# A decoder layer on one core: the loop written out, and the second attention rebuilt

## The chip, the cores and the metric

The kernel runs on one core of a Trainium2 chip. TensorE (PE, with its weight loads, PEld), VectorE (DVE), ScalarE (ACT), GpSimd (POOL) and the DMA queue of SyncE (SP) each follow an instruction list of their own and wait for one another through semaphores. The metric is the device time of one launch in microseconds (us). Most executions of one kernel agree within 0.3%.

## The reference

There are 16 sequences (batches) of 256 tokens with 128 features, everything in fp32. Each goes through three blocks, each followed by a residual sum and a layer norm:

```python
x = _layernorm(x + attn(x))            # 16 heads of 64, causal, distance bias, 2 null keys
x = _layernorm(x + xattn(x, ctx))      # the "second attention": 16 heads of 8, 64 context rows
x = _layernorm(x + ffn(x))             # two matrices without a nonlinearity, 8 groups
# xattn:
qh = einsum('bshd,hed->bshe', q, wq) + bq;  kh = ... + bk;  vh = ... + bv
attn = softmax(einsum('bshd,bthd->bhst', qh, kh) / sqrt(8))
out = (attn @ vh) @ wo.T + bo
```

## The kernel before, in words

A sequence is two tiles (t = 0, 1) of 128 tokens. All engines run one software pipeline of 16 turns, `iteration(i, w, g)`. A turn does the first attention of batch i, the projections of batch i+1, the second attention of batch i-1 and the feed-forward of batch i-1. The order of the work on each engine is written out by hand in `iteration`, and it is strict: an engine that waits holds all that stands behind it. `schedule` writes turns 0, 1, 14 and 15 out; turns 2 to 13 are six passes of a device loop (`Fori`) of two turns. In that loop a wait's value is worked out in registers.

The order on PE in one turn i:

- scores of the first attention in fp32 (L579; heads lie on 64-row halves of the array), with `project_v(i, 6..7)` and `project_qk(i+1, 0..3)` between. A projection is three fp32r products of 512 columns (L462 to L464).
- the first probabilities turned (L599) and weighed (L613), then `weigh_nulls(i, 0)` (L624).
- **the middle of the turn**: `cross_scores(i-1, 0..3)` between `project_qk(i+1, 4..7)`, `cross_values(i-1, 0..1)`, `turn_probs(i, 4..5)`.
- `weigh_values(i, 4..11)`, each with a `turn_probs` behind it. In odd turns a product of the two feed-forward matrices stands between.
- **the tail**: `turn_cross_probs(i-1, 0..3)` (L688), `weigh_cross_values(i-1, 0..3)` (L698), `project_v(i+1, 0..2)`, `x1_turn(i)` and `cross_q(i)` (L638), then `turn_qk(i+1)` (L561) between the last `project_v`, `x2_turn`, `feed_forward`.

How the second attention was done. The queries of head h are 8 rows of `xq`. `spread_context` on POOL multiplies the context keys by a mask into `kexp`, and the values into `vexp`, each 128x1024, so that one product gives the scores of 8 heads. Queries and keys are doubled over the partitions (`xw` has each half of the features twice), as a high and a low fp32r part: ACT writes `xqT_hi` (L1378), DVE the rest `xqT_lo` (L1080). A call `cross_scores(b, k)` (t = k // 2, heads half = k % 2) is two fp32r products of 512 columns, L650 and L652, into bank `psS0` or `psS1`. DVE's `cross_shift` takes the maximum and subtracts it (L1093, L1095). ACT's `cross_exponentials` (L1383), DVE's `cross_denominators` (L1100) and POOL's `norm_cross` (L1564) follow. `cross_values` multiplies the spread values by the output matrix (8 products per batch, L662), ACT copies them to `xv` (L1387), and `weigh_cross_values` sums 16 products of 128x128 (L698) straight into y2, which DVE adds (L1107). `kexp` and `vexp` have one buffer each.

On ACT the middle of a turn is in this order: `copy_qk` 4, 5, 6, `cross_exponentials(0)`, `copy_qk` 7, `square_qk(0, 0)` (L1325), `copy_pT(4)`, `cross_exponentials(1)`, `copy_pT(5)`, `square_qk(0, 1)`, `copy_xv` 0 and 1, `copy_pT(7)`. In the tail: `copy_xpT` 0, `qk_seed(1)`, `copy_xpT` 1, the seed of ln2, `copy_v` 0, `copy_xpT` 2, `copy_v` 1, `copy_xpT` 3, `copy_x1T`, `copy_xqT`.

## Time and profile before

| | us |
|---|---|
| median of 3 runs | 1043.22 |
| lowest and highest | 1042.83, 1047.91 |
| the profiled execution's own time | 1046.49 |
| its span | 1044.6 |
| share of PE, DVE, ACT, POOL | 89%, 79%, 65%, 44% |
| granted TensorE clock, mean | 0.971 |

The page gives, for each engine, the union of the times in which it had an instruction running. An fp32 matmul shows as two records, an fp32r one as one. Ends of matmuls are modelled, so the distance from one start to the next says more than a duration. "Idle before, releaser" is what ended the time in which an engine did nothing; "issue" is idle time for which the profile shows no releaser.

### The profile page before, as it was taken

The page shows a single profiled execution, that of the slowest core. Times are in us where ns is not written, and L with a number is a line of the kernel's source. Part 1 is how long each engine was busy: PE and PEld are TensorE (multiplying, and loading weights), DVE is VectorE, ACT ScalarE, POOL GpSimd, SP SyncE. Part 2 cuts the span into 40 slices and gives each one's busy share as a digit, 9 for nine tenths or more (in the row PEclk, how much of TensorE's full clock was granted, in tenths as well). Part 3 has the DMA queues.
Part 4 walks back from the last instruction along what each step waited for, and adds up shares of the span by engine and source line. Part 5 has one row for each costly group of instructions (what it writes and reads, how often), then busy time and mean ns, then how long its engine had stood idle before and what let it go on. Part 6 is the DMA issues. An engine that isn't in the chain of part 4 may idle for free.

```text
span 1044.6 us, 21679 instructions
## 1 busy us (share of the span) xinstructions
PE 926.9 (89%) x6349; PEld 749.4 (72%) x6349; DVE 826.2 (79%) x2595; ACT 673.8 (65%) x1970; POOL 457.8 (44%) x356
## 2 busy tenths in 40 slices
PE   6887998989899898998979899798989989999785
PEld 5666686868768686786858778586876868777574
DVE  7757788887779877898878888689777987878655
ACT  4764767676575765757667575667747676775642
POOL 0253361826327172552816346172642727264341
PEclk9999999999989998999999999899999999999896
DMA  6000000001000010000100001000010000000000
GB/s 190 6 1 11 1 26 12 6 7 27 14 6 7 11 27 9 7 6 12 26 9 6 12 6 27 14 5 8 8 32 7 7 11 22 6 6 6 6 1 11
DMA packets 26289, 16.24 MB, mean 16 GB/s; under 512 B 3872, under 2 KB 25376, under 8 KB 26144
## 3 DMA queue, kind: packets, MB, share of 16 engines
q1 hardware_dynamic: 26144, 14.52, 4.8%
q8 instruction: 65, 1.06, 0.4%
q14 instruction: 80, 0.66, 0.2%
HBM read 12.41 MB, written 2.10 MB: 14 GB/s over the span
## 4 chain that ended last, share of the span: by engine, by line
PE 51%; DVE 22%; issue 11%; ACT 10%; POOL 3%; DMA 2%; DVEq 0%; ACTq 0%; SPq 0%; POOLq 0%
PE psY L613 11%; PE psS L579 7%; PE psT L599 5%; ACT pr L1353 5%; PE psJ L462 4%; PE psJ L464 3%; PE psJ L463 3%; POOL pr L1557 3%; PE psS L561 3%; PE psS L652 2%; PE psS L698 2%; DVE pr L1029 2%; DVE ssq L982 2%; ACT sq L1325 2%; PE psJ L662 2%
## 5 line engine op out<-in xcount | busy, mean ns | idle before, releaser
L1557 POOL TENSOR_TENSOR pr<-pr,rden 128x512 f32<-128x512 f32 x192 | 193.3, 1040 | 394.1 <-DVE rden L1044 343.9
L1353 ACT ACTIVATE pr<-pr,nmin 128x256 f32<-128x256 f32 (+1 forms) x512 | 225.5, 444 | 12.4 <-DVE nmin L1029 11.7
L1029 DVE CUSTOM_DVE_ANT_0 pr<-psS,alibi,nullmin 128x256 f32<-128x256 f32 (+1 forms) x512 | 183.7, 414 | 46.0 <-PE psS L579 43.2
L613 PE MATMUL psY<-val,pT 128*128 128x128 f32 x1536 | 205.8, 280 | 13.0 <-DVE pT L1053 8.6
L613 PEld LDWEIGHTS psY<-val,pT 128*128 128x128 f32 x1536 | 187.0, 193 | 19.4 <-DVE pT L1053 10.6
L1548 POOL TENSOR_TENSOR qk<-qk,rn 128x1024 f32<-128x1024 f32 x64 | 121.2, 1915 | 85.0 <-DVE x L895 49.6
L579 PE MATMUL psS<-kT,qT 64*128 64x256 f32 (+1 forms) x1024 | 117.9, 363 | 31.6 <-issue 17.4
L599 PE MATMUL psT<-ident,pr 128*128 128x128 f32 x768 | 119.5, 279 | 21.2 <-POOL pr L1557 21.2
L579 PEld LDWEIGHTS psS<-kT,qT 64*128 64x128 f32 x1024 | 82.6, 203 | 62.8 <-DVE nmin L1029 30.8
L599 PEld LDWEIGHTS psT<-ident,pr 128*128 128x128 f32 x768 | 87.9, 142 | 41.4 <-POOL pr L1557 35.6
L1353 ACT ACTIVATION_READ_ACCUMULATOR pr<-pr,nmin 128x1 f32 x512 | 97.1, 190 | 0.0
L1338 ACT ACTIVATE val<-psJ 128x512 f32<-128x512 f32 x112 | 66.3, 594 | 44.7 <-PE psJ L464 42.4
L1368 ACT ACTIVATE pT<-psT 128x512 f32<-128x512 f32 x112 | 66.0, 590 | 23.9 <-PE psT L599 23.1
L462 PE MATMUL psJ<-wqk_hi,xnT_hi 128*128 128x512 f32 x128 | 61.0, 476 | 20.5 <-DVE xnT_lo L976 19.1
L982 DVE TENSOR_REDUCE ssq<-sq 128x16 f32<-128x1024 f32 x64 | 76.3, 1212 | 2.2 <-ACT sq L1325 1.7
L1093 DVE TENSOR_REDUCE xmax<-psS 128x8 f32<-128x512 f32 x64 | 44.0, 688 | 42.7 <-PE psS L652 42.7
L1403 ACT ACTIVATE xpT<-psT 128x512 f32<-128x512 f32 x64 | 37.8, 594 | 61.9 <-PE psT L688 60.6
L1317 ACT ACTIVATE qk<-psJ 128x512 f32<-128x512 f32 x80 | 47.6, 594 | 39.4 <-PE psJ L464 37.6
L1053 DVE COPY pT<-psT 128x512 f32<-128x512 f32 x80 | 54.5, 682 | 19.9 <-PE psT L599 18.8
L698 PEld LDWEIGHTS psS<-xv,xpT 128*128 128x128 f32 x512 | 64.5, 194 | 5.6 <-issue 1.3
L561 PE MATMUL psS<-ident,qk 128*128 128x128 f32 x512 | 67.7, 275 | 0.0
L698 PE MATMUL psS<-xv,xpT 128*128 128x128 f32 x512 | 66.0, 277 | 1.2 <-issue 1.0
(138 smaller groups left out, 1876.2 us busy)
## 6 DMA issues: line engine op xcount, KB each, us to landing
w1s<-w1b SPq DMA_DIRECT2D x8, 258.0 KB, 2.9
xin<-x SPq DMA_DIRECT2D x16, 128.0 KB, 2.2
xres<-x SPq DMA_DIRECT2D x16, 128.0 KB, 2.1
w2s<-w2T SPq DMA_DIRECT2D x8, 256.0 KB, 3.1
out<-x SPq DMA_DIRECT2D x16, 128.0 KB, 1.9
pr<-w_q SPq DMA_DIRECT2D x1, 512.0 KB, 4.3
pr<-w_kv SPq DMA_DIRECT2D x1, 512.0 KB, 4.7
pr<-wvT SPq DMA_DIRECT2D x1, 512.0 KB, 4.1
```

Of the source, the lines that this page charges most:

```text
L462: pe.matmul(dst, hi, whi, start=True, stop=False)
L561: mm = pe.transpose(psS[isk][:, P * j:P * (j + 1)], qk[t][:, col:col + P], ident[:])
L579: mm = pe.matmul(psS[score_bank(t, c)][:, keys * j:keys * (j + 1)], qT[r, h // 2, P * t:P * (t + 1)], kT[r, h // 2, 0:keys], start=True, s ...
L599: mm = pe.transpose(psT[c % 2][:, P * j:P * (j + 1)], pr[t][:, h, P * kt:P * (kt + 1)], ident[:])
L613: mm = pe.matmul(psY[t], pT[c % 4][:, P * j:P * (j + 1)], val[:, kt, P * h:P * (h + 1)], start=(blk == 0), stop=False)
L698: mm = pe.matmul(psS[2][:, P * t:P * (t + 1)], xpT[half][:, P * j:P * (j + 1)], xv[:, 4 * half + j, :], start=(half == 0 and j == 0), stop ...
L982: steps.mark(dve.tensor_reduce(ssq[:, t, H * half:H * (half + 1)], sq[:, HD * half:HD * (half + 1)].rearrange("p (h d) -> p h d", d=DH), A ...
L1029: dve.tensor_tensor_reduce(pr[t][:, h, :], psS[score_bank(t, c)][:, keys * j:keys * (j + 1)], alibi[:, h, SEQ - keys:SEQ], 1.0, nullmin[:, ...
L1338: act.activation(val[:, c // 4, 512 * (c % 4):512 * (c % 4) + 512], psJ[c % 2][:], ACT.Copy).then_inc(v_copied_act, 1)
L1353: act.activation(pr[t][:, h, :], pr[t][:, h, :], ACT.Exp, bias=nmin[:, t, h:h + 1], scale=-1.0, accum_out=dparts[:, t, h, 0:1]).then_inc(e ...
L1548: pool.tensor_tensor(v, v, rn[:, t, H * k:H * (k + 1)].unsqueeze(2).broadcast_to([P, H, DH]), ALU.mult).then_inc(qk_normed, 1)
L1557: pool.tensor_tensor(pr[t][:, hs, :], pr[t][:, hs, :], rden[:, t, hs].unsqueeze(2).broadcast_to([P, heads, P * (t + 1)]), ALU.mult).then_i ...
```

## The change

Two things are changed together. First, `schedule` writes all 16 turns out; no engine has a loop, and all waits are on constants. Second, the second attention is rebuilt:

- Queries and keys stay once over the partitions (8 heads in rows 0 to 63, 8 in rows 64 to 127). `cross_q` is one product, `copy_xqT` one copy, `split_xqT` on DVE is gone. `kexp` is 128x512.
- `cross_scores(b, t)` is two fp32 products on the two row halves, into `psS0` and `psS1`. It needs both banks free.
- `cross_values` and `copy_xv` are gone. `vexp` is 128x256 in two buffers: for each pair of heads a block of 32 columns. `weigh_cross_values(b, t)` is 8 products with 32 weight columns and 128 moving columns, each writing 32 partitions of the bank `psS2`. It waits for both `copy_xpT` of its tile.
- `copy_xoT` on ACT (128x256, after `copy_x1T`) and `merge_cross_heads` on PE (two 128x128 products with the output matrix, after `cross_q`) come ahead of `add_y2`.
- `context_kv` in turn 0 makes the keys with 2 products and the values with 32 small ones, without DVE's `split_context_k`. `shape_of_pairs` writes a mask with five memsets on DVE before turn 0. Three more small DMAs stand in the start.

```diff
-            for i in range(FIRST):
-                iteration(i, i % 2 == 1, (i - 1) // 2)
-            with eng.Fori(0, TURNS) as turn:
-                if steps:
-                    steps.enter_loop(turn, per_turn)
-                for half in range(2):
-                    iteration(2 * turn + (FIRST + half), half == 1, turn + half)
+            for i in range(NB):
+                iteration(i, i % 2 == 1, (i - 1) // 2)
...
             def context_kv():
+                for k in range(2):
+                    take(f'J{k}', kvx_copied, k + 1)
+                    pe.matmul(psJ[k][:], xw[:, 1, :], ctxT_s[:, 512 * k:512 * (k + 1)],
                               start=True, stop=True).then_inc(kvx_ready, 1)
+                for k in range(4):
+                    take(f'J{k % 2}', kvx_copied, k + 3)
+                    for j in range(4):
+                        col = slice(CTX * (4 * k + j), CTX * (4 * k + j + 1))
+                        for half in range(2):
+                            mm = pe.matmul(psJ[k % 2][CTX * half:CTX * (half + 1), P * j:P * (j + 1)],
+                                           ctxT_s[:, col], xw[:, 2, :], start=True, stop=True)
+                    mm.then_inc(kvx_ready, 1)
...
+                pe.matmul(psJ[1][:, 0:SEQ], xw[:, 0, :], x1T[:], start=True, stop=True).then_inc(xqT_ready, 1)
+            def cross_scores(b, t):
+                if t == 0:
+                    pe.wait_ge(xqT_copied, b + 1)
+                    pe.wait_ge(kexp_ready, b + 1)
                 for half in range(2):
+                    take(f'S{half}', xs_sub, XC * b + 2 * t + half + 1)
                 tok = slice(P * t, P * (t + 1))
-                pe.matmul(psS[half][:], xqT_hi[:, half, tok],
-                          kexp[:, half, :, :].rearrange("p h k -> p (h k)"), start=True, stop=False)
-                pe.matmul(psS[half][:], xqT_lo[:, half, tok],
-                          kexp[0:DH, half, :, :].rearrange("p h k -> p (h k)"),
-                          start=False, stop=True).then_inc(xscores_ready, 1)
-            def cross_values(b, c):
-                for j in range(4):
-                    p = 4 * c + j
-                    mm = pe.matmul(psJ[c][:, P * j:P * (j + 1)],
-                                   vexp[:, 2 * p:2 * p + 2, :].rearrange("p h k -> p (h k)"), xwo[:],
-                                   start=True, stop=True)
+                for half in range(2):
+                    r = slice(DH * half, DH * (half + 1))
+                    pe.matmul(psS[half][:], xqT[r, tok], kexp[r, :, :].rearrange("p h k -> p (h k)"),
+                              start=True, stop=True).then_inc(xscores_ready, 1)
...
+            def weigh_cross_values(b, t):
+                if t == 0:
+                    pe.wait_ge(vexp_ready, b + 1)
                     take('S2', h2_added, b + 1)
+                pe.wait_ge(xpT_copied, XC * b + 2 * t + 2)
+                for r in range(2):
+                    for j in range(XH // 4):
+                        mm = pe.matmul(psS[2][32 * j:32 * (j + 1), SEQ + P * t:SEQ + P * (t + 1)], vexp[b % 2][:, j, r, :],
+                                       xpT[j // 2][:, P * (2 * (j % 2) + r):P * (2 * (j % 2) + r + 1)],
+                                       start=(r == 0), stop=(r == 1))
                 mm.then_inc(xpv_done, 1)
+            def merge_cross_heads(b):
+                pe.wait_ge(xoT_copied, b + 1)
+                for t in range(NT):
+                    mm = pe.matmul(psS[2][:, P * t:P * (t + 1)], xoT[:, P * t:P * (t + 1)], xwo[:],
+                                   start=True, stop=True)
+                mm.then_inc(y2_ready, 1)
...
                 if c:
                     cross_scores(i - 1, 0)
                 if a:
                     project_qk(i + 1, 4)
                     project_qk(i + 1, 5)
                     project_qk(i + 1, 6)
                 if c:
+                    cross_scores(i - 1, 1)
                 if a:
                     project_qk(i + 1, 7)
...
                         project_v(i + 1, k)
                     if k == 2:
                         cross_q(i)
+                    if c and k == 0:
+                        weigh_cross_values(i - 1, 0)
+                        turn_cross_probs(i - 1, 2)
+                        turn_cross_probs(i - 1, 3)
+                    if c and k == 1:
+                        weigh_cross_values(i - 1, 1)
                     if k == 1:
                         x1_turn(i)
+                    if c and k == 3:
+                        merge_cross_heads(i - 1)
...
-                split_xqT(i)
...
+            def copy_xoT(b):
+                act.wait_ge(xpv_done, NT * (b + 1))
+                act.activation(xoT[:], psS[2][:, SEQ:2 * SEQ], ACT.Identity, bias=xb[:, 2:3]).then_inc(xoT_copied, 1)
...
                 need(pool, xscores_ready, XC * b)
+                pool.tensor_tensor(kexp[:], hmask2[:].unsqueeze(2).broadcast_to([P, XHALF, CTX]),
+                                   kTx[:, col].unsqueeze(1).broadcast_to([P, XHALF, CTX]),
                                    ALU.mult).then_inc(kexp_ready, 1)
+                need(pool, xpv_done, NT * (b - 1))
+                pool.tensor_tensor(vexp[b % 2][:], xwide[:],
+                                   vx[:, row, :].rearrange("p o (j f) -> p (o j) f", f=32).unsqueeze(2)
+                                   .broadcast_to([P, XH // 4, 2, 32]), ALU.mult).then_inc(vexp_ready, 1)
```

## Rows read from the trace of the kernel before

**Rows 1.** The page: busy time, share of the span and instructions of each engine.
```profile
PE 926.9 (89%) x6349; PEld 749.4 (72%) x6349; DVE 826.2 (79%) x2595; ACT 673.8 (65%) x1970; POOL 457.8 (44%) x356
```
**Rows 2.** Windows from score start to score start: length, busy per engine, granted clock.
```profile
159.78:219.24 59.46, 54.76 (x387) 44.38 (x387) 51.30 (x161) 41.07 (x120) 28.61 (x22) 1.00 0.03 8
219.24:841.94 622.70, 565.73 (x3910) 458.59 (x3911) 510.48 (x1601) 413.83 (x1215) 286.11 (x220) 0.98 0.05 13
841.94:902.17 60.23, 56.01 (x396) 45.60 (x397) 50.74 (x161) 41.65 (x123) 28.63 (x22) 1.00 0.06 17
902.17:961.41 59.24, 54.36 (x386) 44.67 (x387) 48.67 (x151) 40.85 (x118) 28.53 (x22) 1.00 0.02 6
1004.60:1044.60 40.00, 24.96 (x138) 20.65 (x137) 21.96 (x69) 11.45 (x27) 5.99 (x5) 0.80 0.02 7
```
**Rows 3.** Timeline of PE, first loop end: start, length, instruction, idle before.
```profile
282.55 1.16 PE L579 MATMUL psS<-kT,qT 64*128 64x128 f32 x16 [3.36 <-issue]
```
**Rows 4.** Timeline of PE, middle of turn 14.
```profile
920.03 1.13 PE L579 MATMUL psS<-kT,qT 64*128 64x256 f32 x8
921.10 0.66 PE L599 MATMUL psT<-ident,pr 128*128 128x128 f32 x4
...
923.94 0.50 PE L650 MATMUL psS<-kexp,xqT_hi 128*128 128x512 f32 x1
...
924.79 0.50 PE L462 MATMUL psJ<-wqk_hi,xnT_hi 128*128 128x512 f32 x1
...
932.87 1.06 PE L613 MATMUL psY<-val,pT 128*128 128x128 f32 x8
...
943.27 2.05 PE L613 MATMUL psY<-val,pT 128*128 128x128 f32 x16 [1.27 <-DVE pT L1053]
```
**Rows 5.** Timeline of PE, tail of turn 13.
```profile
887.77 1.05 PE L698 MATMUL psS<-xv,xpT 128*128 128x128 f32 x8
888.66 0.60 PE L688 MATMUL psT<-ident,xp 128*128 128x128 f32 x4
...
892.34 1.10 PE L638 MATMUL psJ<-x1T,xw 128*128 128x256 f32 x4
893.28 1.95 PE L698 MATMUL psS<-xv,xpT 128*128 128x128 f32 x16
895.06 1.04 PE L561 MATMUL psS<-ident,qk 128*128 128x128 f32 x8
```
**Rows 6.** Timeline of DVE, middle of turn 14.
```profile
924.90 0.69 DVE L1093 TENSOR_REDUCE xmax<-psS 128x8 f32<-128x512 f32 x1 [1.66 <-PE psS L652]
...
927.58 0.69 DVE L1095 TENSOR_TENSOR xp<-psS,xmax 128x512 f32<-128x512 f32 x1
...
931.88 0.69 DVE L1095 TENSOR_TENSOR xp<-psS,xmax 128x512 f32<-128x512 f32 x1
...
940.56 1.83 DVE L884 SCALAR_TENSOR_TENSOR newt<-newt,ssq 128x32 f32<-128x32 f32 x1
```
**Rows 7.** Timeline of ACT, middle of turn 14.
```profile
930.10 1.05 ACT L1325 ACTIVATE sq<-qk 128x1024 f32<-128x1024 f32 x1
...
933.57 0.58 ACT L1368 ACTIVATE pT<-psT 128x512 f32<-128x512 f32 x1
```
**Rows 8.** Timeline of POOL, middle of turn 14.
```profile
938.57 3.77 POOL L1564 TENSOR_TENSOR xp<-xp,xrden 128x1024 f32<-128x1024 f32 x2
```
**Rows 9.** Groups by line and shape: count, busy us, mean ns, idle before.
```profile
L1557 POOL TENSOR_TENSOR pr<-pr,rden 128x512 f32<-128x512 f32 x192 | 193.3, 1040 | 394.1 <-DVE rden L1044 343.9 <-ACT pr L1353 50.2
L1578 POOL TENSOR_TENSOR kexp<-hmask,kTx 128x1024 fp32r<-128x1024 f32 x16 | 30.4, 1903 | 2.7 <-ACT vTx L1310 2.7
```
**Rows 10.** Timeline of ACT, tail of turn 13.
```profile
887.80 0.58 ACT L1403 ACTIVATE xpT<-psT 128x512 f32<-128x512 f32 x1
```
**Rows 11.** Timeline of DVE, tail of turn 13.
```profile
894.96 0.86 DVE L1080 SCALAR_TENSOR_TENSOR xqT_lo<-psJ,xb,xqT_hi 64x256 fp32r<-64x256 f32 x2
...
896.08 0.67 DVE L1019 COPY qT<-psS 128x512 f32<-128x512 f32 x1
```

More of the change, by code:

```diff
@@ L84, in value @@
     def value(self):
-        return self.n + self.offset
+        return self.n
     def wait(self, eng):
         eng.wait_ge(self.sem, self.value())
-    def enter_loop(self, i, per_turn):
-        self.offset, self.before, self.per_turn = i * per_turn, self.n, per_turn
-    def leave_loop(self, turns):
-        assert self.n - self.before == self.per_turn, ("steps of a turn", self.n - self.before)
-        self.n, self.offset = self.before + turns * self.per_turn, 0
 def chunks_to(chunks, n, c):
@@ L201, in program @@
         x1T = sb("x1T", [P, SEQ])
-        xqT_hi = sb("xqT_hi", [P, 2, SEQ], F32R)
-        xqT_lo = sb("xqT_lo", [DH, 2, SEQ], F32R)
-        kexp = sb("kexp", [P, 2, XHALF, CTX], F32R)
-        vexp = sb("vexp", [P, XH, CTX])
-        xv = sb("xv", [P, XH // 2, P])
+        xqT = sb("xqT", [P, SEQ])
+        kexp = sb("kexp", [P, XHALF, CTX])
+        vexp = [sb(f"vexp{k}", [P, XH // 4, 2, 32]) for k in range(2)]
+        xoT = sb("xoT", [P, SEQ])
         xmax = sb("xmax", [P, NT, XH])
@@ L690, in turn_cross_probs @@
                 mm.then_inc(xprobsT_ready, 1)
-            def weigh_cross_values(b, k):
-                t, half = k // 2, k % 2
-                pe.wait_ge(xpT_copied, XC * b + k + 1)
-                if k == 0:
+            def weigh_cross_values(b, t):
+                if t == 0:
+                    pe.wait_ge(vexp_ready, b + 1)
                     take('S2', h2_added, b + 1)
-                for j in range(4):
-                    mm = pe.matmul(psS[2][:, P * t:P * (t + 1)], xpT[half][:, P * j:P * (j + 1)],
-                                   xv[:, 4 * half + j, :], start=(half == 0 and j == 0),
-                                   stop=(half == 1 and j == 3))
-                mm.then_inc(xpv_done, 1)
+                pe.wait_ge(xpT_copied, XC * b + 2 * t + 2)
[4 more added lines that the diff above has]
+                                       start=(r == 0), stop=(r == 1))
+                mm.then_inc(xpv_done, 1)
+            def merge_cross_heads(b):
[4 more added lines that the diff above has]
+                mm.then_inc(y2_ready, 1)
             def x2_turn(b):
@@ L779, in iteration @@
                     project_qk(i + 1, 4)
+                    project_qk(i + 1, 5)
+                    project_qk(i + 1, 6)
                 if c:
@@ L782, in iteration @@
                 if a:
-                    project_qk(i + 1, 5)
-                    project_qk(i + 1, 6)
-                if c:
-                    cross_scores(i - 1, 2)
-                if a:
                     project_qk(i + 1, 7)
-                if c:
-                    cross_values(i - 1, 0)
-                    cross_scores(i - 1, 3)
-                else:
+                if not c:
                     context_kv()
                 turn_probs(i, 4)
-                if c:
-                    cross_values(i - 1, 1)
                 turn_probs(i, 5)
@@ L835, in iteration @@
                         feed_forward(i - 1, g)
-            schedule(pe, iteration)
+            schedule(iteration)
             b = NB - 1
-            for k in range(XC):
-                cross_scores(b, k)
-            cross_values(b, 0)
+            for t in range(NT):
+                cross_scores(b, t)
             x2_turn(b - 1)
-            cross_values(b, 1)
             feed_forward(b - 1, GROUPS - 1)
@@ L847, in _ @@
             turn_cross_probs(b, 1)
-            pe.wait_ge(h2_added, b)
-            for k in range(4):
-                weigh_cross_values(b, k)
-                if k < 2:
-                    turn_cross_probs(b, k + 2)
+            weigh_cross_values(b, 0)
+            turn_cross_probs(b, 2)
+            turn_cross_probs(b, 3)
+            weigh_cross_values(b, 1)
+            merge_cross_heads(b)
             x2_turn(b)
@@ L1376, in copy_xqT @@
                 act.wait_ge(xqT_ready, b + 1)
-                for half in range(2):
-                    act.activation(xqT_hi[:, half, :], psJ[1][:, SEQ * half:SEQ * (half + 1)], ACT.Identity,
-                                   bias=xb[:, half:half + 1]).then_inc(xqT_copied, 1)
+                act.activation(xqT[:], psJ[1][:, 0:SEQ], ACT.Identity, bias=xb[:, 0:1]).then_inc(xqT_copied, 1)
             def cross_exponentials(b, t):
@@ L1506, in iteration @@
                 copy_x1T(i)
+                if c:
+                    copy_xoT(i - 1)
                 copy_xqT(i)
@@ L1536, in _ @@
                 copy_xpT(b, k)
+            copy_xoT(b)
             ln_seed("ln3", (0, 1), NB)
```

138 lines of the change are left out of this document (45 added, 93 removed).

## The prediction

> **What bounds the kernel now.** I read the page's busy times first [rows 1]: PE is busy 89% of the span, DVE 79%. So the change, which takes work mostly off PE, looks like a large gain. Then I cut the span into turns, from the first score product of one to that of the next [rows 2]. Turn 2, an even turn in the loop that no loop end touches, takes 59.46 us; turn 13, odd, in the loop and also with no loop end behind it, takes 60.23. Turn 14 is written out and takes 59.24. The reader is to see that PE is busy only 54.4 to 56.0 of these, at full clock: some 4 us per turn are PE waits, mostly for DVE, and DVE's own 50 us are in one chain with them. The third view is the time line of each engine in the middle and in the tail of a turn [rows 4 to 8, 10, 11]. There I follow which wait would end last when PE's part gets shorter.
>
> **Part 1, the loop.** The ten turns 3 to 12 take 622.70 us together [rows 2]. Five odd and five even ones without a loop end would take 5 x (60.23 + 59.46) = 598.45. The difference, 24.25 us, is the price of five loop ends, 4.9 each. PE stands 3.36 us at the first of them with no releaser ("issue") [rows 3], and the rest comes behind it: the mean granted clock of the stretch is 0.98 where the turns beside it have 1.00 [rows 2]. Written out, this goes. Bounds: at least 5 x 3.36 = 17, if the lost clock came back for other reasons; at most 25 plus the register work. Of that I find next to nothing: turn 14 (written out, without the load for i+2) is 0.22 shorter than turn 2. I take 0.07 for 12 turns, so 1. The price of the longer code is bounded by the same rows: turn 14 is straight-line code and shows no stall. I take -25.
>
> **Part 2, PE's work in the second attention.** Per turn, from start to start. A `cross_scores` call was 0.85 (923.94 to 924.79) [rows 4], four of them 3.4. The new one has two fp32 products of 512 columns on two row halves. The nearest row is a pair of score chunks: four products of 256 columns on the same halves in 1.07 (920.03 to 921.10) [rows 4], the same columns. Without overlap a record of 256 columns costs 0.235 (four in 0.94, `cross_q`, 892.34 to 893.28) [rows 5], so 8 x 0.235 = 1.9. I take 1.07, since it is the same form, so 2.1 for two. `cross_q` falls from 0.94 to 0.47. `weigh_cross_values` was four times 0.89 (887.77 to 888.66) [rows 5], 3.6, and `cross_values`, eight products of that size, adds 1.8. The new weighing has 8 products of 128 columns per tile: 8 x 0.22 = 1.78 if the four column groups take turns, a quarter of it, 0.45, plus some 0.2 for entering and leaving, if they run side by side. No row shows 32-column weights side by side. I take 0.65, by analogy with the row halves, and keep 1.78 as the other end. `merge_cross_heads` costs two products, 0.45. Sum: 3.4 + 0.94 + 3.6 + 1.8 = 9.7 before, 2.1 + 0.47 + 1.3 + 0.45 = 4.3 after. PE loses 5.4 us of work per turn, 80 us in 15 turns. I expect most of it to turn into waits.
>
> At this place the Trainium skill speaks for and against. "TensorE: Matmul & The Clock Gate" (Part 3, packing small matmuls) states 2.38 times for three column tiles of 32, but also that weight loads overlap running matmuls only when the row group differs, and here all column groups share all rows. By the first, a tile would cost 1.78 / 2.38 = 0.75, an estimate; by the second, 1.78. No run here shows either yet.
>
> **The middle of the turn** (turn 14's times). `cross_scores(0)` starts at 923.94 as before and ends both halves at 925.0, so DVE's first shift starts at 925.1 instead of 924.90 [rows 6]. First shift, denominators and second shift take until 928.4 as DVE's own work (the second ended at 928.27, 927.58 + 0.69 [rows 6]). PE has done `project_qk` 4 to 6 by 927.2 and waits, since `cross_scores(1)` needs both banks: 1.2 us idle. It runs 928.5 to 929.6. Shift 3 then ends about 932.5 (before: 931.88 + 0.69 = 932.57 [rows 6]). `project_qk(7)` ends 930.4. Behind it ACT has, in order, `copy_qk` 7, the squares (1.05 [rows 7]) and `copy_pT(4)`: it ends 932.6, and `weigh_values(4)`, which was at 932.87 [rows 4], starts at 932.65. `cross_exponentials(1)` waits for shift 3, so `copy_pT(5)`, at 933.57 before [rows 7], starts at 933.55. So the 3 us that PE saves here come out as 0.05: two PE waits, 1.2 and 1.4 us. Bounds: +0.9 if the two row halves don't overlap, -2.5 if ACT and DVE had the slack that I don't find.
>
> Then PE is paced by its own weighing until it waits 1.27 for the copy of pT(10) [rows 4]. DVE is late there because its Newton step L884 takes 1.83 (940.56 to 942.39), ending with POOL's two-instruction normalization (938.57 + 3.77 = 942.34) [rows 6, 8]. It is that POOL work which holds it. POOL's `kexp` falls from 1.90 to about 1.04, the price of 128x512 [rows 9], and `vexp` by more. But `norm_cross` waits for DVE's reciprocals, which come some 0.35 earlier (`copy_pT(6)` earlier, since PE's second `cross_values` no longer stands ahead of its transposes). I take -0.35 for this stage, bounds -1.3 (the whole wait goes) and +0.6.
>
> **The tail** (turn 13's times). `weigh_cross_values(0)` now waits for both copies of its tile. The second ends at 887.80 + 0.58 = 888.38 [rows 10], so PE starts at 888.4 instead of 887.77 [rows 5]; 0.65 of work, then both transposes 0.9, 890.0; `project_v(1)` to 890.7. Behind it, on ACT: `copy_v` 1 to 891.3, `copy_xpT` 3 to 891.8. `weigh_cross_values(1)` runs 891.85 to 892.5, then `x1_turn`, `project_v(2)`, `cross_q` (893.9) and the merge (894.3; ACT's two copies ahead of it are done by 893.6). `turn_qk` starts at 894.3 instead of 895.06 [rows 5]. DVE had `split_xqT` for 0.86 [rows 11] ahead of `add_y2` and the first qT copy: without it the copy can start at 895.3, not 896.08 [rows 11]. Both engines agree on -0.75. With column groups one after the other the two weighings cost 2.3 more, of which nothing is hidden: 896.6, so +1.6 instead.
>
> **The sum.** Turns 1 to 14: 14 x (-0.05 - 0.35 - 0.7) = -15. The last 40 us, the chain of the last batch [rows 2]: `split_xqT`, the output product with both `copy_xv`, and part of the weighing at half clock leave it; the merge and `copy_xoT` come in: -3, bounds 0 and -6. Start and turn 0: DVE's splits of the keys and of xqT go, five memsets and 32 small value products (32 x 0.22 = 7 us if none overlap) come in: -1, bounds -4 and +3. Together -25 - 15 - 3 - 1 = -44, against the profiled execution's 1046.5: 1002.5. That execution lay 3.3 above the median. Should the loop ends have cost more in it than in the others, the new kernel has none; otherwise the median is to be scaled. I take 1001.
>
> **The rivals.**
> - Column groups take turns, as the second rule says. For it: no row shows otherwise. Against: the row halves do overlap. The tail is 2.3 worse per turn, 14 x 2.3 = 33: about 1035, from 1028 to 1045.
> - In between: weight loads set the pace, 1.0 per tile, between the two ends. The tail loses 0.7 of its 0.75, 10 us, and start and end 4 more: 1016.
> - PE's saving is realized. For it: PE is the busiest engine [rows 1]. Against: the chains above. If 2.2 more of the 5.4 us came through per turn, 1001 - 31 = 970.
> - Slower: the clock. PE now waits in four more places of each turn, 4 to 5 us in all. In the last 40 us, where PE is busy 62%, the granted clock is 0.80 [rows 2]; in full turns, with 93%, it is 1.00. If each turn gets a stretch at 1.2 GHz behind the waits of the middle and one in the tail, as each loop end has (4.9 less the 3.36 of standing still is 1.5, where only the scores stage is hit), and these reach the dense weighing of 10 us, which at half speed takes 10 more, the turn loses up to 10. It decides from 3 us per turn on, 14 x 3 = 42: then nothing is gained. At 4 us: 1057. Against it: no new wait is longer than 1.5 us, and in the steady turns waits of 1.3 us leave the clock at 1.00.
>
> **Chances.** Forecast 55% (own range 990 to 1012), the in-between 15%, taking turns 14%, PE's saving 10%, clock 6%. The range reaches from the case of 970 to the middle of the taking-turns case: 972 to 1037. A measurement tells 0.5%, 5 us, from no change. Faster than that: all of the forecast, the in-between and PE's saving, and 9 of the 14 for taking turns, 0.89. Same 0.05, slower 0.06.
>
> **What would show it.** No 3 us "issue" gap on PE. Turns of about 58.2. PE busy near 50 us per turn with more idle time, ended by DVE's xp (L1095) ahead of the second cross scores, by ACT's pT ahead of weigh 4, by ACT's xpT ahead of both cross weighings. Weighing starts eight products within 0.5 to 0.7 us if the column groups overlap, within 1.8 if not. The forecast is wrong if `weigh_values(4)` comes over 1 us earlier after `weigh_nulls(0)` than the 8.9 of before, or if the granted clock of full turns is below 1.00.

## The result and the profile after

The changed kernel takes 1009.24 us (median of 5 runs, 1008.33 to 1014.34) against 1045.45 (median of 5) for the kernel before: a ratio of 0.967, 95% interval 0.965 to 0.970. The forecast was 1001, faster. The profiled execution of the changed kernel is the longest of its five, 1014.34 us with a span of 1012.2; the one of before had 1044.6. All times inside the programs below are from such profiled executions, which scatter by some 5 us, most of it before turn 1 (below).

The page first: engines with busy us, share and instructions [rows 1 has before].

```profile
PE 849.9 (84%) x6181; PEld 663.4 (66%) x6181; DVE 802.7 (79%) x2564; ACT 660.7 (65%) x1938; POOL 425.7 (42%) x356
```

PE has lost 77 us of work, twice what the kernel has gained. Windows from score start to score start: turn 2, turns 3 to 12, turn 13, turn 14, turn 15, and what lies behind it (columns as in [rows 2]).

```profile
164.49:222.90 58.41, 49.99 (x373) 39.09 (x373) 50.11 (x159) 40.27 (x118) 26.60 (x22) 1.00 0.03 8
222.90:810.74 587.84, 506.41 (x3771) 396.87 (x3771) 495.70 (x1581) 405.46 (x1195) 266.09 (x220) 1.00 0.05 12
810.74:869.89 59.15, 51.29 (x382) 40.31 (x383) 49.02 (x159) 40.80 (x121) 26.61 (x22) 1.00 0.06 17
869.89:928.31 58.42, 49.95 (x372) 39.09 (x373) 47.43 (x149) 39.96 (x116) 26.56 (x22) 1.00 0.02 6
928.31:980.12 51.81, 39.37 (x294) 30.86 (x294) 28.97 (x113) 27.02 (x93) 17.50 (x16) 0.90 0.01 4
980.12:1012.20 32.08, 14.28 (x72) 8.59 (x72) 18.78 (x56) 7.38 (x17) 5.97 (x5) 0.55 0.03 8
```

Against [rows 2]: turns 3 to 12 fell from 622.70 to 587.84, which is ten plain turns (5 x (58.41 + 59.15) = 587.8); nothing of a loop end is left. A plain even turn fell by 1.05, an odd one by 1.08, though PE works 4.7 us less in each; its idle time rose from 4.7 to 8.4 us. Added up over the span: turns 1 to 14 gave 38.4 us (24.3 for the loop ends, 14.1 for the rest of the turns, of which the first experiment gives some 4 to the loop). All before turn 1 took 5.3 more (105.4 against 100.1), turn 15 and what follows 0.7 more (83.9 against 83.2).

The middle of turn 14 on PE, as in [rows 4], 32.4 us earlier on the clock of the profile:

```profile
891.55 1.13 PE L636 MATMUL psS<-kexp,xqT 64*128 64x512 f32 x4
...
896.22 1.13 PE L636 MATMUL psS<-kexp,xqT 64*128 64x512 f32 x4 [1.00 <-DVE xp L1061]
...
900.45 1.13 PE L600 MATMUL psY<-val,pT 128*128 128x128 f32 x8 [1.33 <-ACT pT L1334]
...
910.70 2.05 PE L600 MATMUL psY<-val,pT 128*128 128x128 f32 x16 [1.09 <-DVE pT L1028]
```

The saved work has become the two waits that were forecast, 1.00 and 1.33 us, and the third wait is still there. The tail of the same turn:

```profile
915.39 0.65 PE L672 MATMUL psS<-xpT,vexp 128*32 128x128 f32 x16 [0.51 <-ACT xpT L1367]
915.97 1.09 PE L660 MATMUL psT<-ident,xp 128*128 128x128 f32 x8
...
918.93 0.64 PE L672 MATMUL psS<-xpT,vexp 128*32 128x128 f32 x16 [1.18 <-ACT xpT L1367]
...
921.47 1.04 PE L548 MATMUL psS<-ident,qk 128*128 128x128 f32 x8
```

Sixteen records, the eight products of a cross weighing, take 0.58 us from start to start (915.39 to 915.97). Both waits for xpT are there. DVE in the middle and the tail of turn 14, beside [rows 6 and 11]:

```profile
907.90 1.92 DVE L859 SCALAR_TENSOR_TENSOR newt<-newt,ssq 128x32 f32<-128x32 f32 x1
...
917.06 1.90 DVE L976 TENSOR_TENSOR nullneg<-nullmul,nullbias 128x64 f32<-128x64 f32 x1
...
920.76 0.69 DVE L989 COPY val<-psJ 128x512 f32<-128x512 f32 x1 [1.56 <-PE psJ L443]
...
927.05 0.69 DVE L994 COPY qT<-psS 128x512 f32<-128x512 f32 x1 [0.98 <-PE psS L548]
```

The Newton step (L859, L884 of before) is as long as it was. In the tail it is now DVE that waits for PE (1.56 and 0.98 us).

### The profile page after: what moved, and what is told of

It reads as the page before. It is cut to its first block, busy times and chain, and to the rows that moved or that the text cites. A ratio compares the mean times of both kernels' runs of the same rounds, so it can differ in the third digit from the quotient of the medians.

```text
span 1012.2 us, 18717 instructions
## 1 busy us (share of the span) xinstructions
PE 849.9 (84%) x6181; PEld 663.4 (66%) x6181; DVE 802.7 (79%) x2564; ACT 660.7 (65%) x1938; POOL 425.7 (42%) x356
## 4 chain that ended last, share of the span: by engine, by line
PE 45%; DVE 25%; ACT 18%; issue 6%; POOL 4%; DMA 2%; DVEq 0%; ACTq 0%; POOLq 0%
PE psY L600 12%; ACT pr L1319 9%; PE psS L566 6%; PE psT L586 5%; PE psS L636 4%; ACT sq L1291 3%; POOL pr L1519 3%; PE psJ L441 3%; PE psS L548 3%; PE psJ L443 2%; PE psJ L442 2%; DVE xp L1061 2%; DVE xmax L1059 2%; DVE ssq L957 2%; ACT xpT L1367 2%
## 5 line engine op out<-in xcount | busy, mean ns | idle before, releaser
L1319 ACT ACTIVATE pr<-pr,nmin 128x256 f32<-128x256 f32 (+1 forms) x512 | 225.3, 443 | 10.8 <-DVE nmin L1004 10.2
L600 PEld LDWEIGHTS psY<-val,pT 128*128 128x128 f32 x1536 | 186.6, 193 | 41.8 <-issue 22.2
L586 PE MATMUL psT<-ident,pr 128*128 128x128 f32 x768 | 116.9, 279 | 20.2 <-POOL pr L1519 20.2
L566 PE MATMUL psS<-kT,qT 64*128 64x256 f32 (+1 forms) x1024 | 111.7, 346 | 19.3 <-DVE nmin L1004 12.9
L566 PEld LDWEIGHTS psS<-kT,qT 64*128 64x128 f32 x1024 | 78.2, 189 | 48.5 <-DVE nmin L1004 19.4
L1304 ACT ACTIVATE val<-psJ 128x512 f32<-128x512 f32 x112 | 66.5, 594 | 25.6 <-PE psJ L443 25.1
L1526 POOL TENSOR_TENSOR xp<-xp,xrden 128x1024 f32<-128x1024 f32 x32 | 60.9, 1902 | 29.2 <-DVE xrden L1068 28.5
L441 PEld LDWEIGHTS psJ<-wqk_hi,xnT_hi 128*128 128x128 f32 x128 | 24.9, 195 | 65.1 <-issue 31.5
```

Source lines behind the costliest of these rows:

```text
L441: pe.matmul(dst, hi, whi, start=True, stop=False)
L566: mm = pe.matmul(psS[score_bank(t, c)][:, keys * j:keys * (j + 1)], qT[r, h // 2, P * t:P * (t + 1)], kT[r, h // 2, 0:keys], start=True, s ...
L586: mm = pe.transpose(psT[c % 2][:, P * j:P * (j + 1)], pr[t][:, h, P * kt:P * (kt + 1)], ident[:])
L600: mm = pe.matmul(psY[t], pT[c % 4][:, P * j:P * (j + 1)], val[:, kt, P * h:P * (h + 1)], start=(blk == 0), stop=False)
L1304: act.activation(val[:, c // 4, 512 * (c % 4):512 * (c % 4) + 512], psJ[c % 2][:], ACT.Copy).then_inc(v_copied_act, 1)
L1319: act.activation(pr[t][:, h, :], pr[t][:, h, :], ACT.Exp, bias=nmin[:, t, h:h + 1], scale=-1.0, accum_out=dparts[:, t, h, 0:1]).then_inc(e ...
```

## The experiments

Each was timed beside the kernel before on one chip; the ratio is to that. Where turns are given, they are read as windows from score start to score start in the run's own profile; from turn 2 to turn 13 they repeat within 0.05 us, even with even and odd with odd, but for a single odd one in some of the kernels. Two of the kernels, one column group and the quarter of the normalization, leave out part of the result; they serve for their times alone.

**The loop alone.** The kernel before with its loop written out.

```
-            with eng.Fori(0, TURNS) as turn:
-                for half in range(2):
-                    iteration(2 * turn + (FIRST + half), half == 1, turn + half)
+            for i in range(NB):
+                iteration(i, i % 2 == 1, (i - 1) // 2)
```

> The kernel before with only its loop over the batches written out; the second attention as it was. My sum has the five loop ends at 24.3 us: their stall of 3.4 us and a stretch at the lower clock behind each, and next to nothing for registers. That gives 24 to 26 us below the kernel before, about 1020, with turns 3 to 12 as long as the others (60.2 odd, 59.5 even), no 3 us gap of PE without a releaser, and the start of turn 1 where it was (100.1 us). Rival A: the longer code costs instruction fetches; then the gain is under 20 us and gaps without a releaser are spread over the turns. Rival B: the start of the changed kernel (5.3 us later at turn 1) is due to the written-out program and not to the second attention: then turn 1 begins 3 to 5 us later here too.

1019.48 us, ratio 0.974 (0.970 to 0.978). Turn 2, turns 3 to 12, turn 13, and turn 15 with all behind it:

```profile
163.20:222.48 59.28, 54.53 (x387) 44.52 (x387) 51.23 (x161) 41.10 (x120) 28.59 (x22) 1.00 0.03 8
222.48:817.62 595.14, 551.33 (x3911) 451.25 (x3911) 506.19 (x1601) 413.77 (x1215) 285.88 (x220) 1.00 0.04 12
817.62:877.36 59.74, 55.73 (x396) 45.73 (x397) 49.98 (x161) 41.62 (x123) 28.58 (x22) 1.00 0.06 17
936.50:1018.10 81.60, 60.26 (x392) 48.58 (x392) 48.53 (x170) 35.79 (x113) 25.50 (x21) 0.85 0.02 6
```

By the medians the loop is 26 of the 36 us. The loop ends are the 24.3 of the forecast, and the plain turns are shorter too, 0.18 even and 0.49 odd against [rows 2], some 4 us where I had 1. I put that down to the register work, the only difference in those turns that I can name; no run separates it. The second attention's edits are then worth 10 us: a pair of turns goes from 119.02 to 117.56, 1.46 less. It lies in the tail (last null weighing to next score start, 16.30 and 16.22 to 15.63); the middle (first to last null weighing) fell by 0.19 in even turns and by nothing in odd ones. Turn 1 begins at 103.6, as in rival B. But seven of the nine profiles listed under the start below, all of written-out kernels, have it between 99.6 and 102.3, so the written-out program alone does not make it 3 to 5 us late.

**One column group.** All products of a cross weighing in the first 32 columns; three quarters of the attended values are left uncomputed.

```
-                for r in range(2):
-                    for j in range(XH // 4):
-                        mm = pe.matmul(psS[2][32 * j:32 * (j + 1), SEQ + ...
+                for j in range(XH // 4):
+                    for r in range(2):
+                        mm = pe.matmul(psS[2][0:32, SEQ + ...
```

> The changed kernel, but the eight products of a cross weighing all go to the first 32 columns of the array, so that none can run beside another (the three other quarters of the attended values are left uncomputed). If the column groups are what makes the weighing 0.58 us from start to start, it becomes 1.7 to 1.8 us per tile, two tiles per turn, and since the tail of a turn is now bound by PE all of it shows, less what covers a wait of 0.5 or 1.2 us: the second wait (1.18) comes from ACT, which also moves later, so +2.0 to +2.4 us per turn, 28 to 34 us in all, about 1040, the same as the kernel before. Rival: the weight loads and not the products set the pace, then a tile takes 0.9 to 1.1 and the kernel 1018 to 1024. Rival 2: such small products cost little in either arrangement, then 1009.

1048.52 us, ratio 1.003 (1.000 to 1.005): slower than the kernel before by a hair. First the two groups of the weighing by line (count, busy us, mean ns, idle before), this kernel's and then the changed kernel's; then this kernel's turn 14.

```profile
L672 PE MATMUL psS<-xpT,vexp 128*32 128x128 f32 x512 | 63.1, 278 | 26.5 <-ACT xpT L1367 26.5
```

```profile
L672 PE MATMUL psS<-xpT,vexp 128*32 128x128 f32 x512 | 21.5, 287 | 26.5 <-ACT xpT L1367 26.5
```

```profile
898.89:959.88 60.99, 52.53 (x372) 41.61 (x373) 47.43 (x149) 40.00 (x116) 26.57 (x22) 1.00 0.02 5
```

A record takes the same 280 ns in both; only their overlap differs. The two weighings of a turn take 1.84 and 1.87 us from start to start instead of 0.58 each, 2.55 more together; the turn is 2.57 longer, all of it in the tail (15.63 to 18.20). So nothing hides the weighing, and the column groups are what makes the rebuilt attention pay: without them it gives back all that the loop had won. "TensorE: Matmul & The Clock Gate" of the Trainium skill (Part 3, "Measured speedup vs the span model") gives 2.38 times for three column tiles; four gave 1.87 / 0.58 = 3.2 here, and the weight loads did not force them one after the other, although all groups share their rows.

**ACT's copy of pT(4) first.**

```
                     copy_qk(i + 1, 7)
-                    square_qk(i + 1, 0, 0)
...
                 copy_pT(i, 4)
+                if a:
+                    square_qk(i + 1, 0, 0)
```

> The changed kernel with ACT's copy of pT(4) ahead of the first squares (1.05 us) instead of behind them. PE's weighing of chunk 4 waits 1.33 us for that copy in every turn. Theory: the middle of a turn is held at its end by DVE and POOL (Newton step blocked until POOL's normalization ends, then the copy of pT(10)), so the 1.0 us won at chunk 4 is given back as a longer wait at chunk 10 (1.09 us becomes about 1.9), and the squares come later for DVE: 0 to -3 us in all, 1006 to 1009. Rival: ACT's order is what ate PE's saving in the middle; then -0.7 to -1.0 us per turn, 10 to 14 us, 996 to 999. Rival 2: the first squares, 0.6 us later, make DVE's sums and the norms late: 0 to +8.

1009.20 us, ratio 0.964 (0.961 to 0.967); turns 58.42 and 59.17, unchanged. PE in turn 14:

```profile
895.59 1.13 PE L600 MATMUL psY<-val,pT 128*128 128x128 f32 x8 [0.39 <-ACT pT L1334]
...
897.99 1.16 PE L600 MATMUL psY<-val,pT 128*128 128x128 f32 x8 [0.84 <-ACT pT L1334]
...
906.77 2.05 PE L600 MATMUL psY<-val,pT 128*128 128x128 f32 x16 [1.08 <-DVE pT L1028]
```

PE's wait of 1.33 us fell to 0.39, and already the next weighing took it back, with a new wait of 0.84 for ACT's copy of pT(5). The wait for pT(10) stayed (1.08 for 1.09), so the theory had the wrong place for it. The copy of pT(5) stands behind the same work of ACT in both orders, the squares and the second exponentials. The place of this one copy is worth nothing; whether ACT's order as a whole ate the middle's saving was not tried.

**A quarter of the normalization.** POOL normalizes the weights of a quarter of the heads; the others stay as they are.

```
-                    pool.tensor_tensor(xp[t][:], xp[t][:], xrden[:, t, :]...
+                    h = XH // 4
+                    pool.tensor_tensor(xp[t][:, 0:h], xp[t][:, 0:h], xrden[:, t, 0:h]...
```

> The changed kernel with POOL's normalization of the second attention's weights cut to a quarter of the heads (the other three quarters stay unnormalized), so that POOL's two instructions take about 1.2 us instead of 3.85. Theory: it is these that hold DVE's Newton step (1.92 us instead of about 0.2) and so the copy of pT(10); PE's wait of 1.09 us there goes, the turn ends 1.0 us earlier: -14 us, about 995. Rival: the wait passes to the next one in line, PE's own weighing or ACT's copy of pT(11): then -0.3 per turn or less, 1005 to 1009.

999.79 us, ratio 0.957 (0.952 to 0.962): -9.4. DVE in turn 14:

```profile
895.35 0.19 DVE L859 SCALAR_TENSOR_TENSOR newt<-newt,ssq 128x32 f32<-128x32 f32 x1
895.58 0.49 DVE L861 SCALAR_TENSOR_TENSOR rn<-newt,seedq 128x32 f32<-128x32 f32 x1
```

and in turn 13:

```profile
837.62 0.19 DVE L857 TENSOR_TENSOR newt<-seedq 128x32 f32<-128x32 f32 x1 [1.50 <-ACT seedq L1247]
```

Even turns fall to 57.27 (-1.14), odd ones stay at 59.17. So POOL's normalization does hold the middle, but of even turns only. In odd ones DVE waits 1.50 for ACT's seed, which stands behind the copies of the merged feed-forward weights. I had read the middle in turn 14 alone and multiplied by 14.

**The normalization in halves**, four instructions of 512 elements.

```
-                    pool.tensor_tensor(xp[t][:], ...)
+                    for hs in (slice(0, XHALF), slice(XHALF, XH)):
+                        last = pool.tensor_tensor(xp[t][:, hs], ...)
```

> The changed kernel with POOL's normalization of the cross weights in four instructions of 512 elements instead of two of 1024: the same work, about 1.04 us each, 4.1 instead of 3.85 in all. The kernel with a short normalization ran its even turns in 57.27 us instead of 58.41 and its odd ones as before, where DVE waits for ACT's seed instead. Theory: a small DVE operation can begin at an instruction's end of POOL, so DVE's Newton step, which took 1.92 us and ended with POOL's second instruction, takes 1.0 or less, and the even turns become 57.3 to 57.9: -4 to -8 us in all, 1001 to 1005. Rival: POOL keeps DVE out across its back-to-back instructions until it goes idle, then the step is as long as before or longer by 0.2: 1009 to 1011.

1009.45 us, ratio 0.965 (0.963 to 0.968).

```profile
907.91 0.97 DVE L859 SCALAR_TENSOR_TENSOR newt<-newt,ssq 128x32 f32<-128x32 f32 x1
908.91 0.97 DVE L861 SCALAR_TENSOR_TENSOR rn<-newt,seedq 128x32 f32<-128x32 f32 x1
```

The first sentence of the theory holds: the step ends with one instruction of POOL, after 0.97. But each of the two DVE operations behind one another waits for one, so both together are as long as before and the turn gains 0.03.

**ACT's copy of xpT(3) ahead of the value copy.**

```
+                if c:
+                    copy_xpT(i - 1, 3)
                 if a:
                     copy_v(i + 1, 1)
-                if c:
-                    copy_xpT(i - 1, 3)
```

> The changed kernel with ACT's copy of the fourth block of turned cross weights (xpT 3) ahead of its copy of the value chunk (copy_v 1). The second cross weighing waits 1.18 us for that copy in every turn, and the tail of a turn is now bound by PE and this copy, no longer by DVE (DVE's qT copy waits for PE). Theory: the weighing comes about 0.6 us (one ACT copy) earlier and what follows it on PE too, since nothing else waits for copy_v 1 but x1_turn, which stands behind the weighing: -0.4 to -0.6 per turn, -6 to -9 us, 1000 to 1003. Rival: DVE holds the end of the turn (its two copies of qT, the third norm's sums between them), then the saving becomes a longer wait in front of the last transposes: 1007 to 1009.

1005.81 us, ratio 0.963 (0.959 to 0.967). Even turns -0.10, odd ones -0.19, but turn 14 -1.00. That is 2.9 in turns 1 to 14; the medians alone, with intervals that overlap, would not tell it. PE in the tail of turn 12:

```profile
794.40 0.64 PE L672 MATMUL psS<-xpT,vexp 128*32 128x128 f32 x16
...
797.07 1.04 PE L548 MATMUL psS<-ident,qk 128*128 128x128 f32 x8
...
799.43 1.09 PE L548 MATMUL psS<-ident,qk 128*128 128x128 f32 x8 [0.62 <-DVE qT L994]
```

The wait for xpT(3) is gone and PE wins 1.0 us up to the transposes, then waits 0.62 for DVE's first qT copy and is slowed behind it. Theory and rival both hold in part: by what came through, PE and DVE end the tail within 0.2 us of each other. In turn 14, which has no batch i+2 to normalize, DVE has the slack and the whole 1.0 comes through.

**PE's value projection into the wait.**

```
-                    if a and k < 3:
+                    if a and k < 2:
                         project_v(i + 1, k)
+                    if a and k == 1:
+                        project_v(i + 1, 2)
```

> The changed kernel with PE's third value projection (0.7 us of work) in front of the second cross weighing instead of behind it, so that PE has work in the 1.18 us in which it waits for ACT. Theory: the tail is bound by PE's own work plus this wait; -0.5 to -0.7 per turn up to cross_q, less what cross_q then waits for ACT's copy of x1 (0.3 to 0.4): -0.3 per turn, -4 us, about 1005; with no cover by ACT the full -0.7, 999. Rival: DVE or ACT hold the end of the turn, then 1009.

1009.18 us, ratio 0.965 (0.963 to 0.968), turns 58.42 and 59.16: nothing. The work filled the wait (1.18 to 0.48), but the weighing's place is set by ACT's copy, and behind x1_turn a new wait of 0.56 for x1T stands where the projection was.

**One buffer for the spread values.**

```
+            def spread_values(b):
+                need(pool, xpv_done, NT * b)
...
+                spread_values(i)
                 x1_plus_bias(i)
```

> The changed kernel with one buffer of spread values instead of two; POOL fills it late in the turn (0.73 us), in front of its addition of the bias to x1, where it has been free since the weighing of the batch before. Theory: the second buffer is there so that the filling may stand ahead of the normalization on POOL (with one buffer in that place POOL would wait for a weighing that waits for POOL itself); POOL has 1.5 us of idle time in front of both the normalization (it waits for DVE's reciprocals) and the place where it goes, so both cost nothing: 1007 to 1011, even and odd turns 58.4 and 59.2. Rival: the filling in front of the normalization makes it late; then one buffer, filled late, is faster by up to 0.7 us in the even turns, 1004 to 1006.

1010.0 us, ratio 0.967 (0.964 to 0.970), no different from the changed kernel; even turns 58.29, 0.12 shorter, odd 59.15. The second buffer is worth nothing where POOL can fill late; it bought only the place.

**The end with idle products.**

```
+            def keep_busy(n):
+                for _ in range(n):
+                    pe.matmul(psY_bank[:, 2 * P:4 * P], ident[:], alibi[:, 0, :], start=True, stop=True)
```

> The changed kernel with idle products (fp32, 256 columns, 0.47 us each at full clock, into an unused part of a bank) in front of PE's long waits in turn 15 and behind it: 6 and 6 in the turn, 6, 1, 5, 1, 1, 1, 6, 1 behind it. In the profile the last 29 us ran wholly at 1.2 GHz and two stretches in turn 15 too, right behind waits of 3.1 and 3.5 us. Theory (this is why the end gave +0.7 instead of my -3): work in place of the waits keeps the granted clock at 2.4 GHz, the transposes, weighings and merges behind turn 15 (9.5 us of PE time on the path at half clock) take half and some 3 to 5 us in the turn come back: -5 to -8 us, 1001 to 1004. Rival: the end is set by DVE, ACT and POOL, the clock of PE is worth 1 us or nothing there, and the filling that overlaps real work costs: 1008 to 1012.

1003.26 us, ratio 0.961 (0.958 to 0.965): -6. Turn 15 and all behind it, in two windows:

```profile
922.48:971.27 48.79, 40.86 (x319) 32.53 (x319) 28.97 (x113) 27.04 (x93) 17.52 (x16) 1.00 0.01 4
971.27:999.90 28.63, 18.54 (x116) 12.53 (x116) 18.77 (x56) 7.05 (x17) 5.99 (x5) 0.96 0.03 10
```

In the changed kernel these were 51.81 at 0.90 and 32.08 at 0.55. Eight transposes of the last batch took there

```profile
991.27 1.97 PE L660 MATMUL psT<-ident,xp 128*128 128x128 f32 x8 [2.55 <-POOL xp L1526]
```

and here

```profile
981.47 1.09 PE L660 MATMUL psT<-ident,xp 128*128 128x128 f32 x8 [1.15 <-POOL xp L1542]
```

So 5.5 to 6.7 us of the end (77.4 against 82.9 to 84.0 in the profiles of the changed kernel and of the variants that leave the end as it is) are the clock: work that does nothing, put into waits, pays there.

In time the rebuilt attention won nothing there: 82.9 to 84.0 us, against 83.2 in the kernel before and 81.6 in the loop-only kernel, where I had 3 less. The granted clock fits. Over turn 15 and all behind it the mean was 0.86 in the kernel before and 0.85 in the loop-only one, which is 23 and 24 us at 1.2 GHz; in the changed kernel it was 0.77, 39 us. PE is busy for 16.2, 14.2 and 22.2 us of these slow stretches. The products take about half as long at the full clock (the transposes above, 1.97 and 1.09), so the clock costs the changed kernel 3 to 4 us more than the two others, an estimate from these figures and about what is missing. The old attention with a filled end was not run.

**The start.** The fills of the pattern first on DVE, and five idle products ahead of the first transposes.

```
+            shape_of_pairs()
             ln1_begin(0)
...
+            for _ in range(5):
+                pe.matmul(psY_bank[:, 2 * P:4 * P], xoT[:, 0:P], xoT[:], start=True, stop=True)
             pe.wait_ge(c_loaded, 16 * 2)
```

> The changed kernel with two edits at its start: the five fills of the block pattern run on DVE in its first 2.8 us, where it waits for the input, not behind the first qT copies; and PE runs five idle fp32 products of 256 columns on a zeroed tile before the first transposes, where it waits for the input until 5.7 us. In the profile of the changed kernel the first projections have 0.43 us from start to start until 17.3 us and 0.24 behind it, and DVE's first mask is 2.1 us late for PE in turn 0. Turn 1 started at 105.4 there but between 99.7 and 101.4 in five other profiles with the same start, so most of my miss at the start is that one execution. Theory: the early products bring the faster clock to the first projections, and turn 1 starts at 96 to 99; the earlier fills give 0.5 to 1.0 us; 1003 to 1006. Rival A: the start is bound by the loads of the weights and DVE's splits: 1007 to 1009. Rival B: products ahead of the real ones push them back at the lower clock: 1010 to 1012.

1007.13 us (1007.07 to 1007.99), ratio 0.964 (0.962 to 0.966): -2.1, less than expected, and the interval overlaps that of the changed kernel. What speaks for a gain is one profile: turn 1 starts at 98.97. With the unedited start it started at 105.4, 101.4, 101.0, 99.7, 101.1, 101.7, 105.5, 99.6 and 102.3 in the profiles of the changed kernel and its variants (the one with a late fill of the values among them). So my miss of 5.3 us is mostly the one execution; their median is 101.4, 1.2 above the only profile of before. (The expectation named five of them and left out 105.5.) What differs between them is the granted clock: the two at 105.4 and 105.5 have 23.9 us at 1.2 GHz before turn 1, the two at 101.7 and 102.3 have 17.1 and 13.7, the other five 10.2; the kernel before had 6.8 and the loop-only kernel 13.7. Turn 0 is 59.73 instead of 60.56 to 62.8; which of the two edits gave it was not separated.

**Three orders.** The copy of xpT(3) as above; DVE's copy of pT(10) ahead of its Newton steps; POOL's second normalization of q and k behind DVE's null scores.

```
+                copy_pT(i, 10)
                 if a:
                     norms(i + 1, 0)
-                copy_pT(i, 10)
...
-                    pool.wait_ge(x1_ready, i + 1)
+                    pool.wait_ge(dve_step, nulls_at[i + 1])
                     norm_qk(i + 1, 1)
```

> The changed kernel with three changes of order and no change of work: ACT's copy of xpT 3 ahead of its copy of the value chunk 1 (as before, alone -3 us), DVE's copy of pT(10) ahead of the Newton steps of the first norms, and POOL's second normalization of q and k waits until DVE has its null scores instead of starting with x1. Alone the first won PE 1.0 us and gave 0.6 to 0.8 of it back as a wait for DVE's first qT copy, since DVE stands 1.0 and 1.6 us in two small operations that end with POOL's. Theory: DVE comes 2.6 us earlier to the value copy, so the tail keeps its 1.0 us, and in even turns the copy of pT(10) no longer stands behind the blocked Newton step, another 1.0: even turns 56.3 to 57.0, odd ones 58.0 to 58.4, -14 to -21 us, 988 to 995. Rival: POOL is now later at its end and the transposes of the second tile of q and k (turn_qk 4) wait for it: even 57.5, odd 58.4, 999 to 1003.

991.73 us, ratio 0.950 (0.948 to 0.952): 17.5 less than the changed kernel, with no work removed; 13.3 of them lie in turns 1 to 14. The three orders were not timed one by one, but for the first. DVE's null scores in turn 13:

```profile
840.78 0.17 DVE L854 TENSOR_SCALAR ln_ve<-ln_mv 128x2 f32<-128x2 f32 x1
...
841.12 0.23 DVE L977 TENSOR_TENSOR nullneg<-nullmul,nullbias 128x64 f32<-128x64 f32 x1
```

and those of the changed kernel's turn 13:

```profile
859.17 1.23 DVE L853 TENSOR_SCALAR ln_ve<-ln_mv 128x2 f32<-128x2 f32 x1
...
860.56 1.81 DVE L976 TENSOR_TENSOR nullneg<-nullmul,nullbias 128x64 f32<-128x64 f32 x1
```

Even turns take 57.33, odd ones 58.3. In odd turns the tail falls to 14.76, in even ones the middle to 20.40, and there the tail stays at 15.67 against the expectation. The row that says why, PE in turn 12, with DVE's late operation ahead of ACT's seed:

```profile
780.45 0.64 PE L673 MATMUL psS<-xpT,vexp 128*32 128x128 f32 x16 [1.57 <-ACT xpT L1369]
```

```profile
777.71 1.59 DVE L964 TENSOR_SCALAR ssq<-ssq 128x32 f32<-128x32 f32 x1
```

POOL's normalization of q and k now runs beside that DVE operation; ACT computes a seed from it and has the copy of xpT(1) queued behind the seed. To put that copy first is the next edit; it was not tried.

**All together.**

> The three changes of order, the filled end (alone -6 us) and the two edits at the start in one kernel. Theory: places apart from each other add up: the orders' gain, -6, and what the start gives, -3 to -5; 978 to 988. Rival: they share waits, above all in turn 15 and turn 0, and the sum is short by 3 us or more: 990 or over.

986.43 us (985.82 to 987.03), ratio 0.944 (0.942 to 0.945), 22.8 below the changed kernel. The parts are 17.5, 6.0 and 2.1, together 25.6; 2.8 are shared. The three orders alone had already brought turn 1 to 98.4 and turn 15 with all behind it to 81.6; here they are 97.9 and 77.4. It is the fastest kernel of the study.

## Why the prediction was right, and where it was off

- **Loop ends, -24.3**: as forecast, from the windows of [rows 2] alone. What the loop costs beside its ends was mis-sized: 1 us forecast, about 4 measured. I read it from one even turn beside turn 14; odd turns lose more (0.49 against 0.18).
- **Column groups, 0.65 per tile**: 0.58. The rival in which they take turns is refuted for this kernel and confirmed as a price: its tail was forecast 1.6 longer than before, and the kernel that forces it is 1.7 longer (18.19 against 16.46). Its time was forecast at about 1035 (1028 to 1045) and came to 1048.5: my sum lacks 8 us anyway, one group costs 2.57 a turn where I had 2.3, and turn 15 with all behind it takes 88.0 us against 83.9.
- **The middle**: both waits came with their forecast places and sizes (1.0 and 1.33 for 1.2 and 1.4). The -0.35 at pT(10) was too much: -0.19 in even turns, 0 in odd ones, where ACT's seed ends the wait and not POOL. Here is the largest part of the miss in the turns.
- **The tail, -0.7**: -0.6. That it ends on both engines at once was right: with PE's wait alone removed a turn wins 0.1 to 0.2, with ACT's, DVE's and POOL's orders changed together the odd turns' tail wins 0.9.
- **Start and end, -4 together**: failed. The end gave nothing. The filled end shows that the clock costs the changed kernel 5.5 to 6.7 us there, with PE's last 32 us at 0.55; that its growth took the whole 3 is argued from the slow stretches above, not shown. I had counted the work removed at half clock, not that the clock can be lower for longer without it. The start, forecast 1 shorter, is 1.2 longer in the median of profiles; the single execution that I compare with has 5.3.
- **The clock rival (turns at 1.2 GHz behind new waits)**: refuted in turns 2 to 14, granted clock 1.00 with waits up to 1.34 us. It was right in kind for turn 15 and the end.
- **PE's saving realized (970)**: of the 4.5 to 4.7 us that PE works less per turn, some 0.7 came through; the rest of the 1.05 is the loop's.

The sum, with these: 1046.5 - 24.3 - 14.1 + 1.2 + 0 = 1009.3 against 1009.24 measured. That it meets to 0.1 is chance, since start and end scatter by 1 us and more between profiles and 1046.5 is one execution. The forecast of 1001 lacked 8: the end 3, the start 2, the turns 2, and the 1.5 that I took off for the median. The 2 for the turns is luck in part: the loop gave 28.3 where I had 25, the rebuilt attention 10 where I had 15, and the two errors nearly cancel.

## What to carry to other kernels

Take turns with different contents apart before multiplying: an even and an odd turn here wait for different engines at the same place, and one of them gave nothing. When an engine's work is removed, list the waits that remain and whose they are; here the orders on ACT, DVE and POOL were worth 17.5 us, more than the whole rebuilt attention. At a kernel's end, where the busiest engine often waits, read its granted clock: less work on it brought nothing here, and idle products in its waits brought 6 us.

## What the runs showed of the hardware

- Eight fp32 products on four column groups that share all 128 rows take 0.58 us, against 1.84 to 1.87 in one group.
- A small DVE operation that meets a running POOL instruction ends with that instruction (1.92 for 0.19 us, 0.97 when the instruction is half as long), and the next one behind it meets the next instruction. Not all are held: the statistics (two in 0.48), the copies out of PSUM (0.69) and the sums over 1024 elements (1.21) run beside POOL in their usual time. "SBUF — State Buffer" of the Trainium skill ("SBUF: two separate sides") has the rule: of a POOL instruction and a DVE one that needs the port pair both share, the first to start holds it for its whole length, and the other waits. The halved instruction shows that the holding is by instruction and not by the stretch in which POOL is busy.
- Idle products in PE's waits held the granted clock at 0.96 where it had been 0.55.
- In the first 12 us of PE's work, from 5.7 to 17.3, the windows show a granted clock of 1.00 while the 512-column products follow each other at 0.43 us and not at 0.24. 0.43 is the pace that they have in the kernel with the edited start where its window reads 0.51. The profile's first record of the clock is at 17.3 us; before it the products' own distance is to be read, not the clock column.
- With the idle products at the start only PE's first product came at a faster pace, and then the slow one set in anyway (0.51 from 8.0 to 14.5 us). The first products there stand 0.31, 0.38 and 0.43 us apart:

```profile
7.77 0.47 PE L442 MATMUL psJ<-wqk_hi,xnT_hi 128*128 128x512 f32 x1 [1.57 <-DVE xnT_lo L955]
8.08 0.59 PE L443 MATMUL psJ<-wqk_lo,xnT_hi 128*128 128x512 f32 x1
8.46 0.63 PE L444 MATMUL psJ<-wqk_hi,xnT_lo 128*128 128x512 f32 x1
8.89 0.64 PE L442 MATMUL psJ<-wqk_hi,xnT_hi 128*128 128x512 f32 x1
```

PE had waited 1.57 us just before them, and the weights' loads took 99% of the DMA time. What let the clock fall is open.
